# First layer of a four-layer image network: second block in 25 rounds a group, with copied rows, and rows loaded in plain runs

## What is computed

```python
def block(x, w1, b1, w2, b2, w3, b3, a, b, c):     # three neighbouring channels in, one out
    xf = triplets(x)                               # (B * 16, 3, 512, 512), mirrored at the ends
    o = a * conv_reflect(xf, w1, b1, 1, 2) + b * conv_reflect(xf, w2, b2, 2, 4) + c * conv_reflect(xf, w3, b3, 4, 8)
    return tanh(o)                                 # 5x5 kernels, dilation 1, 2 and 4

x = x + block(block(gn(x), *first), *second)
# layers 1 to 3: a 3x3 convolution, a 17x17 box mean, a convolution on the Fourier side
```

## Time and profile before

| | us |
|---|---|
| median of 3 runs | 5300.78 |
| lowest, highest | 5299.0, 5303.86 |
| profiled execution | 5308.6 |
| its span, first to last instruction | 5306.8 |

### The profile page before, as it was taken

One profiled execution on the slowest core, in us unless ns is written; L12 is line 12 of the kernel. 1 busy time (PEld: TensorE's weight loads), 2 busy tenths in 40 slices (PEclk: granted clock), 3 DMA queues, 4 the chain that ended last, 5 costly groups with the idle time before them and its releaser, 6 DMA issues. The chain is left out here.

```text
span 5306.8 us, 178754 instructions
## 1 busy us (share of the span) xinstructions
PE 4988.3 (94%) x78653; PEld 2961.4 (56%) x78653; DVE 3369.1 (63%) x6195; ACT 2400.5 (45%) x2999; POOL 1366.5 (26%) x1629
## 2 busy tenths in 40 slices
PE   4999999999999999999999988998777899999998
PEld 2444444444444467777777763433655466666665
DVE  5653453453433555555555547887999688888888
ACT  2222231231221111111111118875999699999997
POOL 0000000000002111111111100001777255555556
PEclk9999999999999999999999999999999999999999
DMA  8777777777766667667676659997887365666554
GB/s 247 241 250 232 236 252 228 237 251 231 233 206 221 206 207 233 209 206 233 207 224 216 207 161 320 326 320 247 307 309 292 120 152 149 152 152 152 150 152 120
DMA packets 366866, 1166.79 MB, mean 220 GB/s; under 512 B 60458, under 2 KB 61097, under 8 KB 287019
## 3 DMA queue, kind: packets, MB, share of 16 engines
q1 hardware_dynamic: 363928, 1152.98, 68.7%
q10 hardware_dynamic: 2162, 2.39, 0.2%
HBM read 683.58 MB, written 453.51 MB: 214 GB/s over the span
## 5 line engine op out<-in xcount | busy, mean ns | idle before, releaser
L682 PE MATMUL c_p<-c_w,wc 128*32 128x512 f16 x55296 | 3017.4, 380 | 25.5 <-DMA c_w<-xs 23.6
L682 PEld LDWEIGHTS c_p<-c_w,wc 128*32 128x32 f16 x55296 | 1761.9, 97 | 1252.5 <-issue 30.4
L742 ACT ACTIVATE c_t<-c_p,cbias,cscale 128x512 f32<-128x512 f32 x512 | 398.4, 778 | 2385.8 <-PE c_p L682 2385.7
L607 DVE TENSOR_TENSOR a_x<-c_t,a_x 128x512 f32<-128x512 f32 x256 | 222.1, 868 | 656.9 <-ACT c_t L742 656.9
L597 DVE TENSOR_SCALAR c_y<-c_t 128x512 f16<-128x512 f32 x256 | 109.4, 427 | 704.1 <-ACT c_t L742 586.9
L1705 PE MATMUL f_P<-f_qh,f_wt 64*64 64x512 f16 x4608 | 545.7, 378 | 1.8 <-DVE f_t L1601 1.8
L1705 PE MATMUL f_P<-f_hl,f_wt 64*64 64x512 f16 x4608 | 545.3, 379 | 0.0
L1866 POOL TENSOR_TENSOR f_y<-f_y,f_x 128x512 f32<-128x512 f32 x256 | 331.1, 1293 | 448.0 <-DVE f_hl L1580 442.0
L1601 DVE SCALAR_TENSOR_TENSOR f_t<-f_P,f_kk,f_ci 128x256 f32<-128x256 f32 x1024 | 423.6, 476 | 11.9 <-PE f_P L1705 7.2
L813 POOL COPY c_y<-c_y 128x16 f16<-128x16 f16 x512 | 87.2, 200 | 1278.0 <-DVE c_y L599 1278.0
L1465 POOL TENSOR_TENSOR e_hl<-e_g,e_hl 128x2048 f16<-128x2048 f32 x63 | 257.2, 4083 | 609.5 <-ACT e_hl L1415 609.5
(11 more groups left out here) (263 smaller groups left out, 5896.5 us busy)
## 6 DMA issues: line engine op xcount, KB each, us to landing
c_w<-xs SPq DMA_DIRECT2D x576, 264.0 KB, 7.8
c_w<-ys SPq DMA_DIRECT2D x576, 264.0 KB, 3.9
d_x<-x SPq DMA_DIRECT2D x128, 1024.0 KB, 7.6
x<-d_x SPq DMA_DIRECT2D x128, 1024.0 KB, 5.1
ys<-c_y SPq DMA_DIRECT2D x576, 132.0 KB
xs<-a_hl SPq DMA_DIRECT2D x70, 1056.0 KB, 11.3
a_x<-in_x SPq DMA_DIRECT2D x256, 256.0 KB, 5.6
a_x<-in_x SPq DMA_DIRECT2D x128, 512.0 KB, 5.0
```

The source lines that it names most:

```text
L607: v.tensor_tensor(xw[:, g, :], tl[:, :], xw[:, g, :], ALU.add).then_inc(c_lo, 1)
L682: t = p.matmul(pg[32 * j:32 * j + 32, :], wu[:, blk, wl, var, di, :], buf[:, bk, xl * PW + PAD + dx:xl * PW + PAD + dx + NW], start=(di == ...
L742: s.activation(tt_[n % 3][:, :], pp[:, n % 4, :], ACT.Tanh, bias=cbias[:, blk:blk + 1], scale=cscale[:, blk:blk + 1]).then_inc(c_act, 1)
```

## The change

Four edits, all in the first layer.

1. **Rounds.** In the second block a group has 25 rounds. For the shifts -2, -1, 1 and 2 the eight rounds of high weights (by high and by low rows) become six: four on `near`, which holds 96 partitions of high rows (-4 to 19) and, in the other 32 partitions, the low rows outside the band (-4 to -1 and 16 to 19), and two on `twice`, which holds the low rows 0 to 15 in 64 partitions and again in the other 64, shifted by three columns, so that one round makes two shifts. DVE makes `near` in two copies and half of `twice` in one, ACT the other half, for the group to come; PE waits for them inside the group. The partitions of a row buffer are ordered by another rule (`slot`) for this. In both blocks the rounds are taken in another order.
2. **Weights.** Weights for the new rounds (`wn`) lie behind `wc` in one tile; POOL makes them in six small copies before the loop.
3. **Loads.** A load brings two groups, with runs of 16,896 bytes a partition where there were 8,448: four DMAs of 32, 16, 8 and 8 partitions take the place of four of 32. They are issued at g = 1 and g = 3.
4. **Store signals.** `c_yd` has one semaphore for each group, and DVE waits at each g for that group of unit u - 2.

```diff
@@ layer0
-        c_ld = [[sem(f"c_ld{i}{j}") for j in range(4)] for i in range(2)]
-        c_yd = [sem(f"c_yd{i}") for i in range(2)]
+        c_ld = [[sem(f"c_ld{i}{j}") for j in range(2)] for i in range(2)]
+        c_yd = [[sem(f"c_yd{i}{j}") for j in range(4)] for i in range(2)]
...
+        def rows_in(e, n):
+            u, g = divmod(n, 4)
+            e.wait_ge(c_ld[u % 2][g // 2], n_win(u))
+            if n >= 2:
+                e.wait_ge(c_pe, n - 1)
+            return win[u % 2][:, 4 * g:4 * g + 4]
...
-                    if u >= 2 and g == 0:
-                        v.wait_ge(c_yd[u % 2], n_ys(u))
+                    if u >= 2:
+                        v.wait_ge(c_yd[u % 2][g], n_ys(u))
...
+                def copies(n):                                            # VectorE
+                    w = rows_in(v, n)
+                    v.tensor_copy(near[n % 2][0:96], w[0:96, :, 0:PW]).then_inc(c_nh, 1)
+                    v.tensor_copy(near[n % 2][96:128], w[64:96, :, PW:RW]).then_inc(c_nl, 1)
+                    v.tensor_copy(twice[n % 2][0:64], w[0:64, :, PW:RW]).then_inc(c_2a, 1)
...
                     for g in range(4):
+                        if doubled(4 * u + g + 1):
+                            copies(4 * u + g + 1)
...
-                    for di, dx in enumerate(DX):
-                        for z, (wl, xl) in enumerate(((0, 0), (0, 1), (1, 0))):
+                    for di in (4, 0, 1, 7, 8):
+                        for wl, xl in ((0, 0), (0, 1), (1, 0)):
+                            four(wu[:, blk, wl, :, di], rows4, xl * PW + PAD + DX[di], start=(di, wl, xl) == (4, 0, 0))
...
+                    for di in (2, 3, 5, 6):
+                        four(wu[:, blk, 1, :, di], rows4, PAD + DX[di])
+                    if not doubled(n):
+                        for di in (2, 3, 5, 6):
+                            for xl in range(2):
+                                t = four(wu[:, blk, 0, :, di], rows4, xl * PW + PAD + DX[di], stop=(di, xl) == (6, 1))
+                        t.then_inc(c_pe, 1)
+                        return
+                    wnear = wn[pr % 2]
+                    p.wait_ge(c_nh, n_copied(n))
+                    p.wait_ge(c_nl, n_copied(n))
+                    for e, di in enumerate((2, 3, 5, 6)):
+                        four(wnear[:, :, e], near[n % 2], PAD + DX[di])
+                    p.wait_ge(c_2a, n_copied(n))
+                    p.wait_ge(c_2b, n_copied(n))
+                    four(wnear[:, :, 4], twice[n % 2], PAD - 2)
+                    t = four(wnear[:, :, 5], twice[n % 2], PAD - 1, stop=True)
...
+                def copies(n):                                            # ScalarE
+                    w = rows_in(s, n)
+                    s.activation(twice[n % 2][64:128, :, PAD - 2:PAD - 1 + NW], w[0:64, :, PW + PAD + 1:PW + PAD + 2 + NW], ACT.Copy).then_inc(c_2b, 1)
...
                     for gp in (0, 1) if p == 0 else (p + 1,):
-                        for h8 in range(2):
-                            e.dma_start(win[half][gp % 2 + 2 * h8:128:4, 4 * g:4 * g + 4].rearrange("p k w -> p (k w)"),
-                                        dram(src, pair(b, gp, 0, 16 * half + 4 * g) + h8 * (8 * VP - RW),
-                                             [[CP, 16], [RW, 2], [1, 4 * RW]])).then_inc(c_ld[half][g], 16)
+                        at = pair(b, gp, 0, 16 * half + 4 * g)
+                        for first, count, off in ((0, 32, 0), (80, 16, RW), (64, 8, 12 * VP - RW), (112, 8, 8 * VP - RW)):
+                            e.dma_start(win[half][first + gp % 2:first + 2 * count:2, 4 * g:4 * g + 8].rearrange("p k w -> p (k w)"),
+                                        dram(src, at + off, [[CP, count], [1, 8 * RW]])).then_inc(c_ld[half][g // 2], 16)
...
-                        if u + 2 < 2 * NU and not late:
-                            load(u + 2, g)
+                        if u + 2 < 2 * NU and not late and g % 2:
+                            load(u + 2, g - 1)
```

More of the change, by code:

```diff
@@ L40, in slot @@
     def slot(row, chan):
-        h8, s = ((1, 0), (0, 0), (1, 1), (0, 1))[row // 8 + 1]
-        v8 = row + 8 * h8 - 16 * s
-        return 8 * (2 * v8 + chan % 2) + 4 * s + 2 * h8 + chan // 2
+        place = row + (36, 20, 0, 0, 0, 0, 4, 4)[row // 4 + 2]
+        return 4 * place + 2 * (chan % 2) + chan // 2
     sel = np.zeros((27, 3, 32, 128), np.float32)
@@ L333, in layer0 @@
         win.append(sb(ctx, "c_w1", [128, 16, RW], F16))
+        near = [sb(ctx, f"c_n{i}", [128, 4, PW], F16) for i in range(2)]
+        twice = [sb(ctx, f"c_2{i}", [128, 4, PW], F16) for i in range(2)]
         pp = ps(ctx, "c_p", [128, 4, 512])
@@ L381, in n_ys, with doubled, n_copied @@
         def n_ys(u):
-            return 16 * sum(8 + 4 * (place(r)[2] in (0, 7)) for r in range(u % 2, u, 2))
+            return 16 * sum(2 + (place(r)[2] in (0, 7)) for r in range(u % 2, u, 2))
         def n_win(u):
-            return 32 * sum(1 + (place(r)[2] == 0) for r in range(u % 2, u + 1, 2))
+            return 64 * sum(1 + (place(r)[2] == 0) for r in range(u % 2, u + 1, 2))
+        def doubled(n):
+            return 4 * NU <= n < 8 * NU
+        def n_copied(n):
+            return n - 4 * NU + 1
+        def rows_in(e, n):
[4 more added lines that the diff above has]
+            return win[u % 2][:, 4 * g:4 * g + 4]
         def table_of(u):
@@ L676, in products, with four @@
                         p.wait_ge(c_act, n - 3)
[L677 to L691 removed]
+                    def four(weights, source, at, start=False, stop=False):
+                        for j in range(4):
+                            bk = 4 * g + j
+                            var = 0 if (half, bk) == (0, 0) else (2 if (half, bk) == (1, 15) else 1)
+                            t = p.matmul(pg[32 * j:32 * j + 32, :], weights[:, var], source[:, j, at:at + NW],
+                                         start=start, stop=stop, tile_position=(0, 32 * j))
+                        return t
```

58 lines of the change are left out of this document (33 added, 25 removed).

## The result

| | before | after |
|---|---|---|
| median of 4 runs, us | 5301.42 | 5456.55 |
| lowest, highest | 5299.0, 5303.86 | 5442.67, 5469.87 |
| profiled execution, its span | 5308.6, 5306.8 | 5444.58, 5442.8 |

The account below looks back on a forecast made before the run. PE was taken to bound the first layer, with the four DMA engines storing ys as second bound of its first block. 5308.6 - 87 + 40 = 5261.6, less 7.8 for the median, gave 5254 us, range 5180 to 5355.

Parts of the forecast that it names:

- Second block, -87: Second block: two rounds fewer, DVE's copies nearly fill the time; 5.834 to 5.50 us a group, between -10 and -111.
- rival (c): Second block: DVE becomes the bound at 5.79 us or more, 5291 to 5331; over 5700 with slow copies; chance 0.12 and 0.03.
- the 0.1 us over PE's 5.40: Second block: DVE's work, with sums delayed by POOL, takes 5.43 us, taken as 5.50, against PE's 5.40.
- The prediction's own sign for that: Second block: evictions 5.5 us apart, with PE waiting on copies of DVE, would show the forecast right.
- Signals, weights, rounds' order: 0: Store signals given nothing, at best 40 us; weights nothing, at most 5 us; order of the rounds nothing.
- What is late next: First block: with the 14.28 us wait for ys gone, the late load stays put and PE arrives earlier to wait.
- Loads, +40: First block: 8-row transfers on half the engines cost 33 to 44 us, taken as +40; 0 or 84 to 115 otherwise.
- 0.51 us a group that SP seemed to have free: First block between images: 8.7% of 5.9 us is free and swallows the loads' extra 0.33 to 0.45 us a group.
- rival (b): First block: the four engines carrying ys become its bound, loads +84 to +115 us and more; 5329 to 5406; chance 0.18.
- the stretch that the prediction priced at 33 to 44 us: First block: about seven units around each image start, where SP has no spare time, 9 to 13 us an image.
- A group with two passes of POOL in DVE's way: Second block: copies meeting two POOL passes in each unit add 0.53 us a group, giving 5.79 us.
- the 2.4 us for a copy at one element a time: Second block: slow end for a 2112-element DVE copy, from L607's 693 ns for 512; 700 ns was taken instead.

Follow-up runs that it names:

- relieving DVE: Kernel with the first block of before and the second of the change, its third VectorE copy moved to ScalarE: 5212.49 us, against 5215.34 without the move.
- both experiments on them: Kernel before with c_yd split by groups: 5302.52 against 5303.12 us; changed kernel with DVE's wait back at g = 0 for all four groups: 5460.07 us.
- the mixed kernel: First block with layout, loads and signals of the kernel before, second block of the changed one, weights moved by ten small DMAs: 5215.34 us, ratio 0.9838.
- the cut by eights: Kernel before with one in four load DMAs cut into two of 8 x 2 rows: 5389.82 us, ratio 1.0165.

## Why the prediction was wrong

**Second block, -87: right in number, not in its parts.** 5.496 us a group against 5.50, -86 us. Copies took 712 ns (700 forecast; the 0.71 us that the prediction has from the Trainium skill, VectorE: DVE Perf Modes, the perf-mode tier table, is as near), the first of them 911 in the mean, through POOL; the copy on ACT took 1.92 us (2.0). L991 was the right row to go by, and rival (c) didn't come. But the 0.1 us over PE's 5.40 was to be DVE's doing, and it wasn't. The prediction's own sign for that, evictions 5.5 us apart with waits of PE on copies, did not come: they are 5.41 us apart, PE waited for no copy, and relieving DVE gained nothing. The 0.09 us a group are 24 us in all, of which some 20 are seen: the two waits for loads (9.4 us) with the lower clock around them, and 7.1 us of issue. The loads, which were forecast to cost this block nothing, cost it 17 us, and the rounds gained 104 of their 111. That the two errors cancelled is luck.

**Signals, weights, rounds' order: 0, right**, the signals by both experiments on them, the order of the rounds to within 7 us by the first block of the mixed kernel, the weights by a start that is 6 us later, of which wide loads alone make some 3 (85.9). What is late next was the load, as was said.

**Loads, +40: the step that failed.** It measured +217 us in the first block of the changed kernel, and +251 alone with the second block's 17. Three things went wrong in it.
First, the extra on half of the engines was held to be swallowed between images, by 0.51 us a group that SP seemed to have free (8.7% of waiting). It was not swallowed: the cut by eights costs +87 us, 30 of it between images, and the whole change 84 us there. SP's waits don't tell: from 600 to 900 us they fell from 26.2 us only to 13.2, so that SP stood 4% of a time in which PE waited for loads again and again. Why the free time is not to be had is not shown; I read it as work that comes in bursts. This is rival (b)'s mechanism near its low price, with a chance of 0.18; the prediction had 84 to 115 us for it and talked it down to 40.
Second, it priced shapes by how many engines they use and nothing else. Where the rows land costs +58 to +60, the change's rows with its narrower DMAs +97, wide runs +24, and the cut itself 66 to 87. Only the cut was a term. In the stretch that the prediction priced at 33 to 44 us the loss is 133.
Third, it had no term for what follows a stall of PE. With the lower clock behind them, 165 us of waiting cost 225.
Three of its sums are off as well. Rival (b) speaks of up to half again on 115 us, 172, but its range of 5329 to 5406 leaves that out; with it the range ends at 5463 and takes in what was measured. A group with two passes of POOL in DVE's way is 5.96 us and not 5.79, if the 0.175 us of the sum before it stand, so the second block's worst end is a loss of 32 us and not a gain of 10. And the 2.4 us for a copy at one element a time don't follow from the row named, which gives 2.9 by proportion. None of them bears on the failed step.
The sum with the right term is 5261.6 - 40 + 217 - 8 = 5431 us, 26 under the median; the profiled execution was itself 12 under its median.

**What would show it** did: the first block ended at 1896.7 instead of some 1720, and the waits of PE on loads were nearly nine times those of before. DVE no longer waited for ys. The late loads themselves, for which PE waited 11.4, 11.8 and 12.3 us at the three later images, are a sixth of PE's waits.

## What to carry to other kernels

In this kernel the price of a load hung on more than its bytes: on how its outermost dimension deals it to the engines, on the partitions it lands in, on its width, and on the stores beside it. Before a layout is changed for the sake of arithmetic, time its loads alone with the old arithmetic. A queue that stands 9% of the time does not show that 9% more transfers fit in, least of all those that use only part of the engines. And where a change has a part that pays and one that doesn't, ask whether they must be in the same stage: here the layout of the second block didn't have to be that of the first, and the split is worth 241 us against the changed kernel and 88 against the one before.

## What the runs showed that I had not expected

- A load that lands in half of the partitions takes 9.1 us to land where it took 7.3 spread over all, +58 us in all, at equal bytes, runs and engines.
- Two kernels whose load patterns have an outermost dimension of 2 take +2047 and +2436 us, though their runs are as many and as long as those of a pattern with an outer 16. Even there, the spread landing is 390 us the cheaper.
- A fifth load DMA for two groups costs nothing (0.9995), the same DMA cut along the other dimension 1.65%. Neither that cut nor the landing place costs the second block anything (5.833 us a group with either, 5.834 without).
- Stores cut so that all engines can take part, in 66 KB pieces, are worse in the kernel before than stores on a quarter of them in 132 KB pieces (+47 us), and better by 186 us beside the changed loads.
- After 3.33 us without work PE ran at clock 0.52 for the next 6 us.
